# Turned outputs and rows of maxima move into the ring of three PSUM banks, and the scores use the second job bank while it is empty

## The chip, the core and the metric

One core of a Trainium2 chip runs the whole kernel as one program. The time is device microseconds of that core, the median over runs. Its engines work side by side, each in the order of its own queue, and wait for each other by semaphores: TensorE (PE, matrix products; it writes only to PSUM), VectorE (DVE), ScalarE (ACT), GpSimd (POOL) and SyncE (SP, which here issues DMAs). PSUM has eight banks of 128 partitions by 512 floats.

## The reference

For 2048 tokens of width 256, four blocks are added to the residual one after the other, each on a layer norm of the running sum:

```python
x = x + cross_attention(layernorm(x), ctx)   # 16 heads of 16, 1601 keys, softmax(scale*(tau*q.k + delta))
x = x + top1_expert(layernorm(x))            # 8 experts of 256x256, one is chosen for each token
x = x + window_attention(layernorm(x), ctx)  # keys within 16 of p_t, times a Gauss bell, tanh(cat @ W_c)
x = x + slot_ffn(layernorm(x))               # top 8 of 64 slots; a small network on the 64 slots
```

The last block needs a sum over all tokens before its output, so it has an end of its own after all tokens are through.

## The kernel before, in words

**Start.** Contexts and weights are loaded, keys and queries are projected in blocks of 512 columns (`BLOCKS`, `project`), and each block is split into three bf16 parts (`split`, or `block_mid` and `low_of`). Gathers (`move_k`, `move_q`, L525 and L533) copy the parts to the stacks from which a score product gets full precision in one pass. `START` is the order of these steps on every engine, `BESIDE` what stands beside the first 78 maxima units. There `("L", 1)` are statistics of the second tile of tokens, `("U",)` the masks of the window (`masks`, L1613 on), which wait for all constants.

**Chunks.** The tokens are cut in four chunks of 512. A chunk has 52 slots (4 groups of heads by 13 tiles of 128 keys) of 4 quarters, so 208 quarters; quarter q is head q % 4 of slot q // 4. In each quarter TensorE makes one score product (L1350, 512 columns), ScalarE its exponential (L848), and TensorE one or two maxima units (L1064, 401 columns), each reduced by VectorE (L1651). These units are for the row maxima of the group of heads that comes next. At the end of each slot comes the product of the exponentials of the slot before with the values (L1148, four heads, eight records). At the end of a group the output is copied to SBUF by ScalarE, turned by TensorE (`turn_o`, the "o") and normalised by VectorE; the 16 columns of maxima of a group are turned too (`max_rows`, the "m") and written as rows (`max_out`).

**Jobs.** While chunk c runs, the rest of the network for chunk c - 1 is done in jobs between the quarters: `behind(c)` on TensorE, VectorE and ScalarE. `JOBS` holds for each job its name, the one before it, how many quarters behind that it may start, and its hold: how many quarters it keeps its bank. ota/otb turn the attention's output, y0/y1 project it, t1, t2, t3 turn normed tokens, router and e0 to e15 are the experts (one product of 512 columns for each two experts of a tile of tokens; VectorE adds its two halves at L1788 in the quarters q + 4 and q + 5), gateT and gb0/gb1 add biases, score, aT, z are the window, h, logits, slots, alphaT the slots. `places()` gives each a quarter (`AT`).

**Banks.** Two banks hold the scores (`ps_e`), one the running output (`ps_o`), five are `ps_m`: a ring of three for maxima units, and two for jobs, which alternate. Before the change the o and m pass through the two job banks too, at fixed quarters (`O_AT` = 6, 58, 110, 162 and `M_AT` = 45, 97, 149, 201): `places()` keeps those free and lets no job span them, and `job_numbers()` counts them in the alternation. Chunk 0 has no jobs behind it, so its scores rotate over three banks, the second job bank (`ps_x`) being the third; chunks 1 to 3 use two.

**Order.** All queues are static. Before a matmul, TensorE waits for the semaphore of whoever read the bank last: `bank_free` for jobs, `max_taken` for the ring, `exp_done` for scores. VectorE handles its maxima, then the job steps of a quarter (`go_on`). It normalised the o two quarters after TensorE turned it, and wrote the m one quarter after, behind the job steps.

## Time and profile before

| | |
|---|---|
| median of 3 runs | 1088.85 us (1088.72 to 1089.68) |
| the profiled execution | 1086.41 us |
| its span, first to last instruction | 1084.4 us |
| TensorE (PE) busy | 978.2 us, 90% |
| its weight loads (PEld) | 390.6 us, 36% |
| VectorE (DVE) busy | 745.5 us, 69% |
| ScalarE (ACT) busy | 571.3 us, 53% |
| GpSimd (POOL) busy | 63.8 us, 6% |
| mean granted TensorE clock | 0.968 of full speed |

Durations in the rows further down come from the profiled execution. Matmuls are pipelined and their records overlap, so the distance between starts says more than a length.
### The profile page before, as it was taken

What the parts mean: (1) busy time and instruction counts of PE and PEld (TensorE: products, weight loads), DVE (VectorE), ACT (ScalarE), POOL (GpSimd) and SP (SyncE); (2) the same over time, 40 slices, a digit from 0 to 9 for tenths busy, and PEclk for the clock granted to TensorE, in tenths of its full rate; (3) what the DMA queues carried; (4) which work ended last, traced back from release to release, by engine and by line L of the source; (5) the groups of instructions that cost most, each with busy time, mean ns of one, the idle gap of its engine ahead of it and who ended that gap; (6) DMA issues with size and microseconds to landing.
All of it is one profiled execution on the core that took longest, in us unless ns stands there. A gap on an engine that the chain in (4) does not pass through costs nothing.

```text
span 1084.4 us, 13614 instructions
## 1 busy us (share of the span) xinstructions
PE 978.2 (90%) x4794; PEld 390.6 (36%) x4794; DVE 745.5 (69%) x1704; ACT 571.3 (53%) x1063; POOL 63.8 (6%) x91
## 2 busy tenths in 40 slices
PE   6799999999889999989889989989989999889986
PEld 3453323323333334423323333423333333334643
DVE  4688888887677777776677777776767764235634
ACT  2456766666454456665445546665445547740330
POOL 3441000000000000000000000000000000100000
PEclk9899999999899989999899989999899989999999
DMA  7936500001000000001000000001000000140022
GB/s 187 200 73 111 121 1 15 16 1 35 1 16 1 16 1 14 3 1 55 1 16 1 15 1 13 3 1 54 1 15 1 0 2 1 40 125 2 1 97 78
DMA packets 33931, 36.19 MB, mean 33 GB/s; under 512 B 6670, under 2 KB 30523, under 8 KB 33603
## 3 DMA queue, kind: packets, MB, share of 16 engines
q1 hardware_dynamic: 32542, 34.17, 12.5%
q10 hardware_dynamic: 1242, 0.90, 0.6%
q8 instruction: 38, 0.62, 0.2%
q0 software_dynamic: 80, 0.26, 0.1%
q14 instruction: 29, 0.24, 0.1%
HBM read 21.55 MB, written 7.35 MB: 27 GB/s over the span
## 4 chain that ended last, share of the span: by engine, by line
issue 51%; PE 30%; DVE 9%; DMA 2%; ACT 2%; POOL 2%; DVEq 2%; SPq 1%; POOLq 0%; ACTq 0%
PE ps_m L1064 7%; PE ps_o L1148 7%; PE ps_e L1350 5%; DVE mx L1651 4%; PE ps_e L1022 2%; DMA xres<-in_x 1%; PE ps_m L1350 1%; SPq L545 1%; PE ps_m L1168 1%; PE ps_m L1298 1%; POOL rstd L684 1%; POOL xres L735 1%; PE ps_m L1301 1%; DVE xn L1643 1%; DMA x<-xres 1%
## 5 line engine op out<-in xcount | busy, mean ns | idle before, releaser
L1651 DVE TENSOR_REDUCE mx<-ps_m 128x1 f32<-128x401 f32 x1024 | 538.3, 568 | 198.0 <-PE ps_m L1064 190.6
L848 ACT ACTIVATE probs<-ps_e 128x512 f32<-128x512 f32 (+1 forms) x763 | 437.1, 598 | 342.2 <-PE ps_e L1350 340.5
L1064 PE MATMUL ps_m<-k_stack,q_stack 99*128 99x401 bf16 x1024 | 319.4, 343 | 36.6 <-DVE mx L1651 34.9
L1350 PE MATMUL ps_e<-q_stack,k_stack 101*128 101x512 bf16 (+1 forms) x763 | 299.5, 394 | 10.9 <-ACT probs L848 8.7
L1148 PE MATMUL ps_o<-probs,v_heads 128*32 128x512 f32 (+1 forms) x1664 | 228.9, 623 | 0.0
L1350 PEld LDWEIGHTS ps_e<-q_stack,k_stack 101*128 101x128 bf16 (+1 forms) x763 | 75.9, 100 | 261.8 <-ACT probs L848 167.7
L1064 PEld LDWEIGHTS ps_m<-k_stack,q_stack 99*128 99x128 bf16 x1024 | 102.0, 100 | 183.8 <-DVE mx L1651 131.0
L1252 PE MATMUL ps_m<-expert_w,xnT 128*128 128x512 f32 x192 | 99.4, 598 | 15.2 <-DVE xb L1788 15.2
L1148 PEld LDWEIGHTS ps_o<-probs,v_heads 128*32 128x32 f32 (+1 forms) x1664 | 33.1, 109 | 60.7 <-issue 49.4
L848 ACT ACTIVATE probs<-ps_m 128x512 f32<-128x512 f32 (+1 forms) x69 | 41.6, 603 | 15.2 <-PE ps_m L1350 15.1
L1788 DVE SCALAR_TENSOR_TENSOR xb<-ps_m,hot,xb 128x256 f32<-128x256 f32 x84 | 40.6, 484 | 7.9
L1252 PEld LDWEIGHTS ps_m<-expert_w,xnT 128*128 128x128 f32 x192 | 34.2, 191 | 30.6 <-DVE xb L1788 20.4
L682 POOL TENSOR_TENSOR var_e<-mv,eps 128x4 f32<-128x4 f32 x13 | 2.6, 199 | 573.9 <-DVE mv L1737 566.6
L1403 PE MATMUL ps_m<-expert_w,xnT 128*128 128x512 f32 x64 | 29.0, 598 | 1.3 <-DVE xb L1953 1.3
L1350 PE MATMUL ps_m<-q_stack,k_stack 101*128 101x512 bf16 (+1 forms) x69 | 26.4, 383 | 0.0
L735 POOL TENSOR_TENSOR xres<-xres,bo 128x1024 f32<-128x1024 f32 x3 | 7.1, 2354 | 253.7 <-DMA xres<-in_x 253.7
L1022 PE MATMUL ps_e<-xnT,expert_w 128*128 128x512 f32 x32 | 17.2, 623 | 2.0 <-DVE work L1575 1.3
L1953 DVE SCALAR_TENSOR_TENSOR xb<-ps_m,hot,xb 128x256 f32<-128x256 f32 x28 | 13.5, 484 | 7.5 <-PE ps_m L1403 5.6
L1403 PEld LDWEIGHTS ps_m<-expert_w,xnT 128*128 128x128 f32 x64 | 11.7, 190 | 14.5 <-issue 11.0
L1298 PE MATMUL ps_m<-win_v,work 128*128 128x256 f32 x48 | 14.5, 383 | 1.5 <-ACT work L858 1.5
L1201 PE MATMUL ps_m<-ident,xn 128*128 128x128 f32 x72 | 15.0, 292 | 0.0
L1168 PE MATMUL ps_m<-wc,ident 128*128 128x512 f32 x24 | 14.6, 749 | 0.4 <-ACT alphaT L968 0.4
(333 smaller groups left out, 720.0 us busy)
## 6 DMA issues: line engine op xcount, KB each, us to landing
q_stack<-q_parts SPq DMA_DIRECT2D x78, 64.0 KB, 2.6
expert_w<-in_expert_wT SPq DMA_DIRECT2D x2, 1024.0 KB, 12.9
xres<-in_x SPq DMA_DIRECT2D x4, 512.0 KB, 3.8
x<-xres SPq DMA_DIRECT2D x4, 512.0 KB, 3.2
probs<-x SPq DMA_DIRECT2D x1, 2048.0 KB, 8.5
k_stack<-alphaT SPq DMA_DIRECT2D x10, 200.1 KB, 7.6
probs<-in_ctxT SPq DMA_DIRECT2D x3, 512.0 KB, 7.5
q_parts<-probs SPq DMA_DIRECT2D x4, 384.0 KB, 3.0
```

Source lines behind the costliest of these rows:

```text
L735: pool.tensor_tensor(xres[:], xres[:], bo0[:].unsqueeze(1).broadcast_to((P, TT, D)), ALU.add)\
L848: act.activation(probs[0:n, k % 2, h, :], score_bank(c, k, h)[0:n, :], ACT.Exp).then_inc(s["exp_done"], 1)
L1022: mm = pe.matmul(ps_e[b % 2][:, 0:n], wqkv[:, w, k, P * m:P * m + P], src[:, k, at_col:at_col + n], start=(k == 0), stop=(k == KT - 1))
L1064: pe.matmul(ps_m[:, (UNITS * n1 + u) % RING, 0:SPLIT], qst[0:MAX_ROW, g, h, P * t:P * t + P], kst[0:MAX_ROW, HG * g + h, QUARTER_START[q]: ...
L1148: mm = pe.matmul(ps_o[32 * h:32 * h + 32, :], v_sb[0:n, st, HG * g + h, :], probs[0:n, k % 2, h, :], start=(st == 0), stop=(st == ST - 1))
L1168: pe.matmul(out, ident[:], wc[:, 0:KT, :], start=True, stop=True)
L1252: mm = pe.matmul(bank(name, c), xnT[:, k, P * t:P * t + P], expert_w[:, k, CT * j:CT * j + CT], start=(k == 0), stop=(k == KT - 1))
L1298: pe.matmul(o, aT[:, k, tok:tok + P], win_v[:, k, :], start=(k == 0), stop=False)
L1350: pe.matmul(score_bank(c, k, h)[0:n, :], kst[0:ROWS, HG * g + h, P * st:P * st + n], qst[0:ROWS, g, h, :], start=True, stop=True).then_inc ...
L1403: mm = pe.matmul(half_bank(f"e{i}", h), xnT[:, k, tok:tok + P], expert_w[:, k, CT * j:CT * j + CT], start=(k == 0), stop=(k == KT - 1))
L1651: dve.tensor_reduce(mx[:, q, col:col + 1], ps_m[:, (UNITS * n1 + u) % RING, 0:SPLIT], AX.X, ALU.max)\
L1788: last = dve.scalar_tensor_tensor(out=xb[:, t, :], in0=bank(f"e{i}", c)[:, D * (e % 2):D * (e % 2) + D], scalar=hot8[:, t, e:e + 1], in1=( ...
```

## The change

The o and the m become items of the ring of three: `ring_numbers()` counts them in one order with the maxima units, the same on TensorE and VectorE, and both wait and signal on the ring's semaphores `max_ready` and `max_taken`. `places()` loses its fixed quarters, and `job_numbers()` its m and o. VectorE handles the m and the o in the quarter in which TensorE turns them, ahead of the job steps of that quarter. `score_plan()` chooses for every score of all chunks the bank whose last score is longest ago: out of three when no job holds the second job bank or takes it in the next quarter, else out of the two `ps_e`. A score in the third bank waits that the last job there is taken; a job in that bank waits for the exponential of the last score there.

At the start the first block of queries is projected before the third and fourth block of keys, the gathers of the first 1024 columns of keys go in two pieces of 512, the first by SyncE alone, and the first normalisation comes after the first block of keys on ScalarE. The second tile's statistics and the masks are done before the first maximum; the two constants that the masks need are loaded early under a semaphore of their own, and GpSimd's `scale_shift(1)` is moved with them.

```diff
-BLOCKS = ([("K", i, 0) for i in range(N_COLS)] + [("Q", 0, 0), ("Q", 0, 1)] + [("K", i, 1) for i in range(N_COLS)]
+BLOCKS = ([("K", 0, 0), ("K", 1, 0), ("Q", 0, 0)] + [("K", i, 0) for i in range(2, N_COLS)] + [("Q", 0, 1)]
+          + [("K", i, 1) for i in range(N_COLS)]
...
-HALVES = ((0, 2 * CT, 1), (2 * CT, S, N_COLS - 1))
-GATHER_SP, GATHER_ACT = (0, 4, 2), (1, 5, 3)
-START = [("D",), ("L", 0), ("C",), ("N", 0), ("K", 0, 0), ("S",), ("K", 1, 0), ("T", 0), ("K", 2, 0), ("K", 3, 0), ("G", 0),
-         ("Q", 0, 0), ("g",), ("G", 1)]
-START += [("V", i) for i in range(V_EARLY)]
+KEY_PIECES = ((0, CT, ("K", 0, 0)), (CT, 2 * CT, ("K", 1, 0)), (2 * CT, S, ("K", N_COLS - 1, 0)))
+HALF_OF_PIECE = (0, 0, 1)
+GATHER_SP = ((0, 4, 2, 1, 5, 3), (0, 4, 2, 1), (0, 4, 2))
+GATHER_ACT = ((), (5, 3), (1, 5, 3))
+START = [("D",), ("L", 0), ("C",), ("K", 0, 0), ("N", 0), ("S",), ("K", 1, 0), ("T", 0), ("Q", 0, 0), ("G", 1), ("K", 2, 0), ("g",),
+         ("K", 3, 0), ("V", 0), ("V", 1), ("G", 2)]
+START += [("V", i) for i in range(2, V_EARLY)] + [("L", 1), ("U",)]
...
 def places():
-    fixed = sorted([(q, q + 3) for q in O_AT] + [(q, q + 2) for q in M_AT])
     ring, at = [(0, 0), (0, 0)], {}
     for name, after, lag, hold in JOBS:
-        q = at[after] + lag if after else lag
-        while True:
...
+        q = max(at[after] + lag if after else lag, ring[-2][1])
...
 def job_numbers():
+    order = [(name, c) for c in range(NC - 1) for name in AT]
+    return {job: (1 - i % 2, i // 2) for i, job in enumerate(order)}
+
+def ring_numbers():
+    order = []
+    for v in range(UNITS + LEAD):
+        if v == UNITS + 3:
+            order.append(("m", 0))
+        order.append(divmod(v, UNITS))
     for c in range(NC):
         for q in range(HG * SLOTS):
+            k, h = divmod(q, HG)
+            order += [(NG * c + j, u) for j, u in units_at(k, h) if wanted(NG * c + j)]
             if q in M_AT and wanted(NG * c + 1 + M_AT.index(q)):
                 order.append(("m", NG * c + 1 + M_AT.index(q)))
             if q in O_AT and (c or q > O_AT[0]):
                 order.append(("o", NG * c + O_AT.index(q) - 1))
...
+def score_plan():
+    hold = {name: h for name, _, _, h in JOBS}
+    jobs = [(HG * SLOTS * (c + 1) + AT[name], name, c) for name, c in JOB if JOB[name, c][0] == 1]
+    plan, last, last_score = [], [None] * 3, {}
+    for n in range(HG * SLOTS * NC):
+        near = any(at <= n + 1 and n < at + hold[name] for at, name, _ in jobs)
+        b = min(range(2 if near else 3), key=lambda i: -1 if last[i] is None else last[i])
+        begun = [(name, c) for at, name, c in jobs if at < n]
+        plan.append((b, last[b], begun[-1] if begun else None))
+        last[b] = n
+        last_score.update({(name, c): last[2] for at, name, c in jobs if at == n})
+    return plan, last_score
...
         def bank_free(eng, job, c):
             b, n = JOB[job, c]
             need(eng, bank_taken[b], n)
+            if b and LAST_SCORE[job, c] is not None:
+                eng.wait_ge(s["exp_done"], LAST_SCORE[job, c] + 1)
...
         def score_bank(c, k, h):
-            return ps_e[h % 2] if c else (*ps_e, ps_x)[(HG * k + h + 1) % 3]
+            return (*ps_e, ps_x)[SCORES[HG * (SLOTS * c + k) + h][0]]
...
+            sp.dma_start(iota_w[:], io["c_iota"].partition_broadcast(P)).then_inc(s["ld_masks"], 16)
+            sp.dma_start(slotT[:], io["slot_initT"].rearrange("(k p) n -> p k n", p=P)).then_inc(s["ld_masks"], 16)
...
             pool.memset(eb[:], 0.0).then_inc(s["fills_set"], 1)
+            scale_shift(1)
...
                     for h in range(HG):
-                        need(pe, s["exp_done"], HG * SLOTS * c + HG * k + h - (1 if c else 2))
+                        b, last, job = SCORES[HG * (SLOTS * c + k) + h]
+                        if last is not None:
+                            pe.wait_ge(s["exp_done"], last + 1)
+                        if b == 2 and job:
+                            wait_taken(pe, *job)
...
             def masks():
-                dve.wait_ge(s["ld_const"], N_CONST)
+                dve.wait_ge(s["ld_masks"], 32)
...
                                 if u == UNITS - 1:
                                     max_columns()
-                        if h == 0 and st == 2 and (g or c):
+                        if HG * k + h in M_AT and wanted(NG * c + max_end(k - 1)):
+                            j = max_end(k - 1)
+                            need(dve, m_loaded[(j - 1) % NG], 32 * (c + (j - 1) // NG + 1))
+                            max_out(NG * c + j)
+                        if HG * k + h in O_AT and (g or c):
                             if g == 1 and c:
                                 wait_filled(dve, "y1", c - 1)
                             normalise(NG * c + g - 1)
                         go_on(work, HG * k + h)
```

## Rows read from the trace of the kernel before

**Rows 1.** busy time by stage, its first line naming the columns
```profile
core 0: us, PE busy (x) PEld busy (x) DVE busy (x) ACT busy (x) POOL busy (x), PEclk, DMA share, GB/s
...
91.50:250.00 158.50, 154.87 (x888) 47.53 (x888) 133.49 (x276) 109.07 (x211) 0.61 (x1) 1.00 0.22 41
250.00:493.00 243.00, 222.56 (x1123) 85.83 (x1119) 176.46 (x393) 133.06 (x243) 5.98 (x7) 0.96 0.04 11
493.00:734.80 241.80, 221.11 (x1123) 85.04 (x1119) 176.10 (x392) 132.73 (x243) 5.98 (x7) 0.97 0.04 12
734.80:966.00 231.20, 209.98 (x1052) 79.39 (x1048) 136.00 (x311) 132.33 (x243) 8.33 (x8) 0.96 0.04 13
```

**Rows 2.** waits in the stretch 493:734.8: us in total, times, longest
```profile
DVE mx L1651 <- PE ps_m L1064: 56.4, 67, 2.7
...
PE ps_m L1064 <- DVE mx L1651: 9.8, 18, 1.8
...
PE ps_m L1252 <- DVE xb L1788: 5.1, 4, 1.6
```

**Rows 3.** timeline, a slot with experts: start us, us, instruction
```profile
335.68 0.39 PE L1350 MATMUL ps_e<-q_stack,k_stack 101*128 101x512 bf16 x1
...
337.50 0.38 PE L1350 MATMUL ps_e<-q_stack,k_stack 101*128 101x512 bf16 x1
...
337.53 1.06 DVE L1651 TENSOR_REDUCE mx<-ps_m 128x1 f32<-128x401 f32 x2
338.68 0.48 DVE L1788 SCALAR_TENSOR_TENSOR xb<-ps_m,hot,xb 128x256 f32<-128x256 f32 x1
...
339.24 1.07 PE L1148 MATMUL ps_o<-probs,v_heads 128*32 128x512 f32 x8
340.24 0.39 PE L1350 MATMUL ps_e<-q_stack,k_stack 101*128 101x512 bf16 x1
```

**Rows 4.** timeline, TensorE at an expert that waits for its bank
```profile
561.74 1.12 PE L1252 MATMUL ps_m<-expert_w,xnT 128*128 128x512 f32 x2 [1.51 <-DVE xb L1788]
```

**Rows 5.** timeline, hand-overs at quarters 13 and 18 of chunk 2
```profile
504.31 0.38 PE L1350 MATMUL ps_e<-q_stack,k_stack 101*128 101x512 bf16 x1
...
504.67 0.58 ACT L858 COPY attn_chunk<-ps_m 128x512 f32<-128x512 f32 x1
...
511.54 0.38 PE L1350 MATMUL ps_e<-q_stack,k_stack 101*128 101x512 bf16 x1
...
511.68 0.68 DVE L1725 TENSOR_TENSOR xa<-xres,ps_m 128x512 f32<-128x512 f32 x1
```

**Rows 6.** timeline, bare slots at the end of chunk 3
```profile
927.80 0.70 PE L1350 MATMUL ps_e<-q_stack,k_stack 101*128 101x512 bf16 x2
...
928.94 0.88 PE L1350 MATMUL ps_e<-q_stack,k_stack 101*128 101x512 bf16 x2 [0.44 <-ACT probs L848]
...
930.75 0.61 PE L1350 MATMUL ps_e<-q_stack,k_stack 101*128 101x512 bf16 x2
```

**Rows 7.** busy time of a slot of chunk 2 with maxima and statistics
```profile
694.20:698.30 4.10, 3.21 (x21) 0.77 (x17) 4.01 (x13) 2.28 (x4) 1.21 (x2) 1.00 0.00 0
```

**Rows 8.** timelines and busy time around the masks
```profile
33.86 0.58 DVE L1651 TENSOR_REDUCE mx<-ps_m 128x1 f32<-128x401 f32 x1 [10.44 <-PE ps_m L1064]
...
41.73 0.34 PE L1064 MATMUL ps_m<-k_stack,q_stack 99*128 99x401 bf16 x1 [0.83 <-DVE mx L1651]
...
53.66 0.52 PE L1064 MATMUL ps_m<-k_stack,q_stack 99*128 99x401 bf16 x1 [4.39 <-DVE mx L1651]
...
53.66:58.50 4.84, 4.65 (x9) 2.21 (x10) 4.17 (x13) 0.37 (x1) 1.81 (x5) 0.50 1.06 150
```

**Rows 9.** DMA issues by shape: count, KB each, median us to landing
```profile
k_stack<-k_stack SPq DMA_DIRECT2D x3, 128.0 KB, 6.7
...
k_stack<-k_stack SPq DMA_DIRECT2D x3, 72.1 KB, 4.9
```

**Rows 10.** busy time of the stretch that holds the wait at 561.74
```profile
558.00:575.00 17.00, 14.65 (x75) 5.15 (x68) 10.76 (x22) 7.96 (x15) 0.00 (x0) 1.00 0.00 1
```

More of the change, by code:

```diff
@@ L149, in places @@
 def places():
-    fixed = sorted([(q, q + 3) for q in O_AT] + [(q, q + 2) for q in M_AT])
     ring, at = [(0, 0), (0, 0)], {}
     for name, after, lag, hold in JOBS:
-        q = at[after] + lag if after else lag
-        while True:
-            while fixed and fixed[0][0] < q:
-                ring.append(fixed.pop(0))
-            q = max(q, ring[-2][1])
-            if not fixed or fixed[0][0] >= q and ring[-1][1] <= fixed[0][0]:
-                break
-            q = max(q, fixed[0][0] + 1)
+        q = max(at[after] + lag if after else lag, ring[-2][1])
         at[name] = q
@@ L180, in job_numbers @@
                 order.append(("o", NG * c + O_AT.index(q) - 1))
-        if c == 0:
-            first = len(order)
-        else:
-            order += [(name, c - 1) for name in AT if AT[name] >= HG * SLOTS]
     order.append(("o", NG * NC - 1))
-    numbers = {job: (0, i) for i, job in enumerate(order[:first])}
-    numbers.update({job: (1 - i % 2, i // 2 + (first if i % 2 else 0)) for i, job in enumerate(order[first:])})
-    return numbers
+    return {item: i for i, item in enumerate(order)}
 def begin(steps):
@@ L398, in build @@
         k_loaded = [sem(f"k_loaded{g}") for g in range(NG)]
-        k_half = [sem(f"k_half{i}") for i in range(len(HALVES))]
+        k_half = [sem(f"k_half{i}") for i in range(2)]
         q_loaded = [sem(f"q_loaded{g}") for g in range(NG)]
@@ L611, in _ @@
                 sp.wait_ge(q_stored[m], 16 * NC)
-            for half in k_half:
-                sp.wait_ge(half, 16 * K_PARTS)
+            for i, half in enumerate(k_half):
+                sp.wait_ge(half, 16 * K_PARTS * HALF_OF_PIECE.count(i))
             sp.wait_ge(k_loaded[1], 16 * K_PARTS)
@@ L1057, in max_unit @@
                 if n1 == 0 and u % (UNITS // 2) == 0:
[L1058 removed]
+                    half = u // (UNITS // 2)
+                    pe.wait_ge(k_half[half], 16 * K_PARTS * HALF_OF_PIECE.count(half))
                 if u == 0:
@@ L1070, in max_rows @@
                 pe.wait_ge(s["mx_ready"], n1 + 1)
-                bank_free(pe, "m", n1)
-                filled(pe.transpose(bank("m", n1)[0:HG * TT, 0:P], mxc[:], ident[:]), "m", n1)
+                ring_free(pe, ("m", n1))
+                pe.transpose(ring_bank(("m", n1))[0:HG * TT, 0:P], mxc[:], ident[:]).then_inc(s["max_ready"], 1)
             def step(kind, *args):
@@ L1462, in _ @@
             for b in range(2):
-                pe.wait_ge(bank_taken[b], 1 + max(n for bank_no, n in JOB.values() if bank_no == b))
-            pe.wait_ge(s["max_taken"], UNITS * NG * NC)
+                pe.wait_ge(bank_taken[b], sum(bank_no == b for bank_no, _ in JOB.values()))
+            pe.wait_ge(s["max_taken"], len(RING_NO))
             turned_half("ot", 0, att)
@@ L1659, in max_out @@
             def max_out(n1):
-                wait_filled(dve, "m", n1)
-                dve.tensor_scalar(mrow[:, 0, :], bank("m", n1)[0:HG * TT, 0:P], -1.0, None, ALU.mult)
+                wait_ring_filled(dve, ("m", n1))
+                turned = ring_bank(("m", n1))[0:HG * TT, 0:P]
+                dve.tensor_scalar(mrow[:, 0, :], turned, -1.0, None, ALU.mult)
                 dve.drain()
-                taken(dve.scalar_tensor_tensor(out=mrow[:, 1, :], in0=bank("m", n1)[0:HG * TT, 0:P], scalar=-1.0,
-                                               in1=mrow[:, 0, :], op0=ALU.mult, op1=ALU.subtract), "m", n1)
+                dve.scalar_tensor_tensor(out=mrow[:, 1, :], in0=turned, scalar=-1.0, in1=mrow[:, 0, :],
+                                         op0=ALU.mult, op1=ALU.subtract).then_inc(s["max_taken"], 1)
             def step(kind, *args):
@@ L1714, in normalise @@
                         dve.wait_ge(k_loaded[g], 16 * k_loads(g))
-                turned = bank("o", n).rearrange("p (t j e) -> p t j e", t=TT, j=HG)
+                turned = ring_bank(("o", n)).rearrange("p (t j e) -> p t j e", t=TT, j=HG)
                 dve.reciprocal(z_inv[:], turned[:, :, :, E])
```

85 lines of the change are left out of this document (45 added, 40 removed).

## The prediction

> **What bounds the kernel now.** I read the busy time by stage first. From 91.5 us on, four chunks of 52 slots take 158.5, 243.0, 241.8 and 231.2 us, and TensorE is busy 98, 92, 91 and 91% of them; VectorE is behind it with 73%, ScalarE with 55% [rows 1]. So TensorE sets the time, and what can change is its stalls and the stretches at the lower clock. The waits of one chunk name two kinds that end at VectorE: 18 waits for a maxima bank, 9.8 us, and 4 waits for an expert's bank, 5.1 us [rows 2]. The timeline says what a slot (four quarters) looks like while experts run: one slot from 335.68 to 340.24 is 4.56 us, filled but for the last tenth, with its values product of 1.07 us at the end [rows 3]. The same rows hold what matters most here: the third quarter's score starts at 337.50, but VectorE ends the second quarter's expert work only at 338.68 + 0.48 = 339.16, after two maxima of 1.06 us. VectorE runs 1.66 us behind TensorE at that point, and it costs nothing, since no one asks for that bank before the next quarter but one.
>
> **The plan that comes out of the change.** Following the planner's rules with the fixed places gone: e2 moves from quarter 48 to 46, e5 from 64 to 60, e13 from 98 to 92, gb0 from 112 to 104, and everything after it is 8 quarters earlier. Of the 208 scores of a chunk with jobs behind it, 41 go to the third bank. The rule takes the bank whose last score is oldest, so the third bank is taken at once when its job's hold has passed: an expert at quarter q has hold 6, and the score at q + 6 goes there. It waits for that expert's bank to be taken, which VectorE does in quarter q + 5. For e6, e8, e10, e12 and e14 (64, 72, 80, 88, 96) that score is at 70, 78, 86, 94 and 102, each the third quarter of a slot: exactly the place of the row at 337.50.
>
> **Chunks 1 to 3, new waits.** Each of the five costs 339.16 - 337.50, with the release some 1.7 us: 8.5 us. The row says such a wait is real: an expert that asks one quarter after the last take of its bank, at 561.74, stood 1.51 us for it [rows 4]. The score at 62 waits for e4, by the same rows about 1.4, since TensorE has there done a turned output more. The score at 48 waits for e1 behind a values product of 1.07 us [rows 3] (0.4 left), gb1 at 106 for e15 (1.7 less 0.39 for the score and maxima ahead of it: 1.3), the score at 108 for gb0 (0.3). Sum 11.9 us a chunk; bounds 8.5 and 14, because a VectorE that is ahead by one finished wait could shave the next.
>
> The other hand-overs of the third bank ask in the same way one quarter after the take. In today's trace the score at quarter 13 starts at 504.31 and ScalarE's copy of ota ends at 505.25 (0.9 us); at quarter 18 the score starts at 511.54 and the sum of y0 ends at 512.36 (0.8) [rows 5]. t1a at quarter 31 is a copy as ota's. With the release, 1.0, 0.9 and 0.9. Five more of this shape (router at 35, score0 at 125, z0 at 151, t3a at 173, slots at 201) I estimate at 0.5 to 1.0 each, 3.5 together. Where a wait for the same engine follows closely, part is paid already: I take 5.5 of 6.3. Bounds 2 (VectorE is the slower one around them anyway) and 7.
>
> **What goes.** The four expert waits: e2, e5 and e13 no longer come behind an m; e4 moves from the third to the first quarter of a slot, behind a values product of 1.07 us, which covers it. That is -5.1 us a chunk [rows 2]. The wait of gb0 (-0.5) and ota's wait for the output normalised two quarters later (-0.3) go with it. The third bank elsewhere: without it the score at 928.94 stands 0.44 us behind an exponential, and the slot from 927.80 to 930.75 takes 2.95 us [rows 6]; with one more bank the fourth score waits where the third does, 0.5 us less a slot. Where maxima run, the free slots are VectorE's: 4.01 us busy of 4.10 [rows 7], so a third bank buys little; I take -1.5 a chunk over some 8 slots. In chunk 3 maxima end at slot 36, and nine slots gain 0.5 more: -4.5 there. Bounds of what goes: -5 and -9.
>
> The o and m items now take two places of the ring's order. VectorE handles o two quarters earlier and stands for the transposes; the next maxima, and with them TensorE's ring, are queued behind it. It idles 56.4 us of the chunk for maxima [rows 2], so this costs 0; without that cover it is about 0.5 us for each of four. The bank's wait on exponentials asks for a score at least two quarters old, done by then: 0. Since each new wait gives VectorE time, I take 1 us a chunk off the 9.8 us of ring waits.
>
> Net: 11.9 + 5.5 - 5.1 - 0.8 - 1.5 - 1.0 = +9.0 for chunks 1 and 2, +4.5 for chunk 3: **+22.5 us**. Chunk 0 already rotates three banks: 0.
>
> **Before the chunks.** The masks and the second tile's statistics move ahead of the first maximum, where VectorE is idle for 10.44 us waiting for it; the work is about as long as the two stalls below, and hides there. In the loop they made TensorE stand 4.39 us at 53.66 and 0.83 at 41.73, and after the first the granted clock was 0.50 for the 4.84 us from 53.66 to 58.50, which costs half of that, 2.4 [rows 8]. Sum -7.6, and the row of maxima one unit earlier -0.4: **-8**. What is late next is VectorE's own maxima, 78 x 0.5 us, with some 4 us of slack over the shortened loop. The new order of blocks readies the first queries some 3 us earlier (two blocks of keys, each a pass of VectorE over 512 columns, come behind them now), but the first maximum starts with the last gather, and there are now 12 key pieces of 64 KB in place of 6 of 128 KB. A gather of 128 KB lands in 6.7 us and one of 72 KB in 4.9 [rows 9]: halving the size saves a quarter of the time and doubles the number, up to 3 us later; the earlier queries give up to 3 back. I take 0, bounds -3 and +3. SyncE also issues two loads (mask indices, slots) earlier, 1.2 us ahead of gathers that wait for another store anyway. Bounds of the whole part: -11 and 0.
>
> The Trainium skill, page "DMA: Bandwidth & Descriptors", section "Why small descriptors are slow (HBM only)", says that transfers from SBUF to SBUF don't suffer from small pieces. By it the split gathers would cost nothing and the first maximum would be up to 3 us earlier; the two rows on the gathers disagree with it in part.
>
> **Sum.** +22.5 - 8 = +14.5 us on the profiled execution's 1086.41 us (span 1084.4), 1100.9. That run was 2.4 us under the median of the timed ones, so I expect **1103 us**. With all bounds one way: chunks +1, start -11, about 1079; the other way +43 and 0, about 1132. Its own range is 1090 to 1118.
>
> **Rivals.**
> - *The third bank pays and its waits are covered (faster), 0.19.* If VectorE comes to the expert work sooner than today, so that each new wait is half as long (6.0), and the hand-overs lie in slots that VectorE sets anyway (1.0), a chunk is 6.0 + 1.0 - 8.4 = -1.4, chunk 3 -5.9, and with -8 it is -17: 1072 to 1080, say 1075. For it: the row of 4.01 of 4.10. Against: the two maxima that delay the expert's take are issued by TensorE only in the quarter just before. The point from which it decides: new waits below 12.6 us a chunk of my 17.4.
> - *The clock falls in the expert stretch (slower still), 0.10.* If half of the 18 expert waits are each followed by a stretch like that after 53.66 (4.84 us at half clock, 2.4 us lost), +22: 1125. For it: 4.39 us of idle was followed by one. Against: waits of 1.5 us in the stretch from 558 to 575 ran at 1.00 throughout [rows 10]. The Trainium skill, page "TensorE: Matmul & The Clock Gate", section "A second HAM failure mode: psum-queue depth-cycling", describes just this: a kernel that cycles PSUM banks idles briefly so often that the clock swings. By that rule it is 1125, by the row nothing.
> - *The change doesn't do what it says, 0.02*: third-bank scores too few to show, the start alone, 1081.
>
> The forecast has 0.69. The range 1085 to 1119 holds it nearly whole and a small part of the first rival. A difference of 0.2% (2.2 us) is about what can be told from none: faster 0.19, within 0.04, slower 0.77.
>
> **What would show it.** Right: score matmuls (L1350's line) idle for VectorE's expert sum, 18 times about 1.5 us; expert products waiting for an expert's bank nearly gone; slots 17 to 25 alternating 4.6 and about 6.2 us; the first score some 8 us before 91.5, at about 83.5; bare slots of chunk 3 at 2.4 us. Wrong: if slots 17 to 25 stay at 4.6 us, the new waits are not there and the first rival holds; if the mean granted clock of chunks 1 to 3 falls below today's 0.96 to 0.97 by more than 0.02, the second.

## The result and the profile after

The changed kernel took 1118.97 us (median of 4 runs, 1118.25 to 1122.76) beside 1089.03 for the kernel before on the same chip: a ratio of 1.0281, 95% interval 1.0257 to 1.0305. It is slower, as forecast, but by 30 us where 14.5 were forecast: at the upper edge of the range of 1085 to 1119, and just above the forecast's own 1090 to 1118. The profiled execution of after took 1118.63 us, its span is 1116.6, so 32.2 us of span have to be found against before's 1084.4.

Busy time by stage of the kernel after, from its first score on; the columns are as in [rows 1]:

```profile
88.30:248.50 160.20, 156.75 (x890) 46.60 (x889) 134.21 (x277) 109.74 (x212) 1.09 (x1) 1.00 0.22 41
248.50:505.20 256.70, 223.06 (x1123) 85.84 (x1119) 176.76 (x393) 133.26 (x243) 6.00 (x7) 0.96 0.03 9
505.20:761.70 256.50, 222.88 (x1123) 85.27 (x1119) 176.82 (x393) 132.97 (x243) 5.99 (x7) 0.96 0.04 11
761.70:999.40 237.70, 206.10 (x1036) 78.21 (x1032) 136.92 (x312) 130.52 (x241) 8.34 (x8) 0.96 0.04 13
```

TensorE's work in chunks 1 and 2 is the same to 2 us (222.6 and 221.1 before), as is VectorE's. The stages grew by waiting, 13.7 and 14.7 us. The last chunk of [rows 1] was drawn to 966, 2.3 us past its last score; by score to score it was 228.8, so chunk 3 grew by 8.8.

The waits of TensorE in chunk 2 of the kernel after, to be held against [rows 2] (us in total, times, longest). L1394 is the score, L1104 the maxima product, L1833 the expert sum, L1292 the expert product, L1197 the turned output:

```profile
PE ps_m L1394 <- DVE xb L1833: 10.7, 7, 1.8
PE ps_m L1104 <- DVE mx L1695: 10.0, 17, 1.8
PE ps_m L1394 <- ACT xnT L897: 1.8, 2, 0.9
PE ps_m L1394 <- ACT hT L943: 1.6, 1, 1.6
PE ps_m L1197 <- DVE mx L1695: 1.2, 2, 1.0
...
PE ps_m L1394 <- DVE slot_acc L1911: 1.1, 1, 1.1
PE ps_m L1394 <- ACT attn_chunk L897: 0.9, 1, 0.9
PE ps_m L1394 <- DVE lg L1799: 0.9, 1, 0.9
PE ps_m L1394 <- DVE xa L1770: 0.8, 1, 0.8
PE ps_m L1394 <- ACT work L935: 0.7, 1, 0.7
...
PE ps_m L1394 <- DVE work L1770: 0.5, 1, 0.5
PE ps_m L1292 <- DVE xb L1833: 0.2, 1, 0.2
```

Every row of L1394 with a reader other than the exponential is a score in the third bank: 19.0 us in 16 waits, seven of them behind experts. The expert product's own wait, 5.1 in [rows 2], is 0.2. The ring's wait for maxima stayed, 10.0 against 9.8.

One such wait on the timeline of the kernel after, in the third quarter of a slot as in [rows 3]:

```profile
601.43 0.38 PE L1394 MATMUL ps_e<-q_stack,k_stack 101*128 101x512 bf16 x1
601.44 0.48 DVE L1833 SCALAR_TENSOR_TENSOR xb<-ps_m,hot,xa 128x256 f32<-128x256 f32 x1
601.65 0.51 PE L1104 MATMUL ps_m<-k_stack,q_stack 99*128 99x401 bf16 x2
601.85 0.60 ACT L887 ACTIVATE probs<-ps_e 128x512 f32<-128x512 f32 x1 [0.59 <-PE ps_e L1394]
602.02 1.06 DVE L1695 TENSOR_REDUCE mx<-ps_m 128x1 f32<-128x401 f32 x2
603.17 0.48 DVE L1833 SCALAR_TENSOR_TENSOR xb<-ps_m,hot,xb 128x256 f32<-128x256 f32 x1
603.80 0.38 PE L1394 MATMUL ps_m<-q_stack,k_stack 101*128 101x512 bf16 x1 [1.64 <-DVE xb L1833]
```

VectorE takes half of the expert at 601.44, then two maxima, then the other half at 603.17; only 0.15 us after that has ended does the score start. The profile calls 1.64 us idle; the slot as a whole is 1.80 longer than one without it. From score to score, slots 15 to 25 of chunk 2 took 6.36, 4.56, 6.36, 4.56, 6.36, 4.56, 6.36, 4.56, 8.20, 5.00 and 6.37 us: the alternation that the forecast named. The 8.20 is the wait at quarter 94 with a stretch at half clock behind it.

The start. TensorE's first maxima on its timeline, in the kernel before and in the kernel after:

```profile
33.50 0.50 PE L1064 MATMUL ps_m<-k_stack,q_stack 99*128 99x401 bf16 x2
36.25 0.83 PE L1104 MATMUL ps_m<-k_stack,q_stack 99*128 99x401 bf16 x2 [7.79 <-DMA q_stack<-probs]
```

From there to the first score it is 52.0 us, before 58.0. So the masks' stalls of [rows 8] did go, but 2.75 us of the gain was paid before the loop: the first score is at 88.27 instead of 91.51.

### The profile page after: what moved, and what is told of

It reads as the page before. It is cut to its first block, busy times and chain, and to the rows that moved or that the text cites. A ratio compares the mean times of both kernels' runs of the same rounds, so it can differ in the third digit from the quotient of the medians.

```text
span 1116.6 us, 13781 instructions
## 1 busy us (share of the span) xinstructions
PE 974.1 (87%) x4794; PEld 386.3 (35%) x4794; DVE 746.5 (67%) x1704; ACT 571.5 (51%) x1063; POOL 64.4 (6%) x91
## 4 chain that ended last, share of the span: by engine, by line
issue 50%; PE 29%; DVE 8%; DMA 4%; SPq 3%; ACT 2%; POOL 2%; DVEq 1%; POOLq 0%; ACTq 0%
PE ps_m L1104 7%; PE ps_o L1188 7%; DVE mx L1695 5%; PE ps_e L1394 5%; PE ps_m L1394 2%; DMA xres<-in_x 2%; PE ps_e L1061 1%; SPq L578 1%; DMA q_stack<-probs 1%; DMA d_parts<-delta_parts 1%; POOL rstd L721 1%; POOL xres L773 1%; PE ps_m L1341 1%; DVE xn L1687 1%; PE ps_m L1338 1%
## 5 line engine op out<-in xcount | busy, mean ns | idle before, releaser
L887 ACT ACTIVATE probs<-ps_e 128x512 f32<-128x512 f32 (+1 forms) x640 | 370.3, 599 | 293.3 <-PE ps_e L1394 291.7
L1104 PE MATMUL ps_m<-k_stack,q_stack 99*128 99x401 bf16 x1024 | 318.9, 343 | 40.3 <-DVE mx L1695 30.9
L1394 PE MATMUL ps_e<-q_stack,k_stack 101*128 101x512 bf16 (+1 forms) x640 | 249.3, 391 | 2.5 <-ACT probs L887 2.3
L1104 PEld LDWEIGHTS ps_m<-k_stack,q_stack 99*128 99x128 bf16 x1024 | 101.4, 99 | 194.4 <-DVE mx L1695 136.4
L887 ACT ACTIVATE probs<-ps_m 128x512 f32<-128x512 f32 (+1 forms) x192 | 115.1, 599 | 101.0 <-PE ps_m L1394 100.8
L1394 PEld LDWEIGHTS ps_e<-q_stack,k_stack 101*128 101x128 bf16 (+1 forms) x640 | 64.1, 100 | 199.7 <-ACT probs L887 116.4
L1394 PE MATMUL ps_m<-q_stack,k_stack 101*128 101x512 bf16 (+1 forms) x192 | 75.7, 394 | 56.2 <-DVE xb L1833 32.1
L1292 PE MATMUL ps_m<-expert_w,xnT 128*128 128x512 f32 x192 | 99.8, 601 | 0.7 <-DVE xb L1833 0.7
L1394 PEld LDWEIGHTS ps_m<-q_stack,k_stack 101*128 101x128 bf16 (+1 forms) x192 | 19.2, 100 | 123.0 <-issue 61.8
L1833 DVE SCALAR_TENSOR_TENSOR xb<-ps_m,hot,xb 128x256 f32<-128x256 f32 x84 | 40.6, 483 | 7.8
L1292 PEld LDWEIGHTS ps_m<-expert_w,xnT 128*128 128x128 f32 x192 | 35.1, 193 | 12.5 <-DVE xb L1833 2.1
L1061 PE MATMUL ps_e<-xnT,expert_w 128*128 128x512 f32 x32 | 17.3, 628 | 2.9 <-issue 2.9
L1998 DVE SCALAR_TENSOR_TENSOR xb<-ps_m,hot,xb 128x256 f32<-128x256 f32 x28 | 13.6, 484 | 7.5 <-PE ps_m L1447 5.6
L813 ACT ACTIVATE work<-ps_e,cond 128x512 f32<-128x512 f32 (+1 forms) x11 | 7.2, 653 | 21.0 <-PE ps_e L1061 21.0
L1447 PEld LDWEIGHTS ps_m<-expert_w,xnT 128*128 128x128 f32 x64 | 11.7, 190 | 14.4 <-issue 11.0
L1338 PE MATMUL ps_m<-win_v,work 128*128 128x256 f32 x48 | 14.5, 383 | 1.6 <-issue 1.6
```

Source lines behind the costliest of these rows:

```text
L887: act.activation(probs[0:n, k % 2, h, :], score_bank(c, k, h)[0:n, :], ACT.Exp).then_inc(s["exp_done"], 1)
L1061: mm = pe.matmul(ps_e[b % 2][:, 0:n], wqkv[:, w, k, P * m:P * m + P], src[:, k, at_col:at_col + n], start=(k == 0), stop=(k == KT - 1))
L1104: pe.matmul(ring_bank((n1, u))[:, 0:SPLIT], qst[0:MAX_ROW, g, h, P * t:P * t + P], kst[0:MAX_ROW, HG * g + h, QUARTER_START[q]:QUARTER_STA ...
L1292: mm = pe.matmul(bank(name, c), xnT[:, k, P * t:P * t + P], expert_w[:, k, CT * j:CT * j + CT], start=(k == 0), stop=(k == KT - 1))
L1338: pe.matmul(o, aT[:, k, tok:tok + P], win_v[:, k, :], start=(k == 0), stop=False)
L1394: pe.matmul(score_bank(c, k, h)[0:n, :], kst[0:ROWS, HG * g + h, P * st:P * st + n], qst[0:ROWS, g, h, :], start=True, stop=True).then_inc ...
```

## The experiments

All times are compared with the kernel before, run on the same chip; across chips its median was 1087.0 to 1089.0. Chunk lengths are from first score to first score in each profiled run (the last one to its last score). "Half clock" is a granted clock of 0.50; where a stretch is bound by TensorE, a microsecond of it costs up to 0.5 us against full clock.

**e1: the scores keep two banks.** What is left of the change is the ring with o and m in it, the new places, and the start.

```diff
-        near = any(at <= n + 1 and n < at + hold[name] for at, name, _ in jobs)
+        near = n >= HG * SLOTS
```

> The kernel after, but in chunks 1 to 3 the scores use their own two banks alone; o and m stay in the ring, the start is the new one. Theory H (the third bank costs the time: each first score in it behind a job waits for the job's last reader): all hand-over waits go, 20.9 us in chunk 2 of the trace after, while what stays of the change is the start (-3.2), chunk 0 (+1.7), the waits of pairs and experts for the expert sum that are gone (-5.1 in each of chunks 1 to 3) and the ring's new waits (+1.6 in each); about 1089 - 3.2 + 1.7 + 3 x (-3.5) = 1077 us, between 1072 and 1082, and PE's idle in front of scores put down to the expert sum below 1 us in a chunk. Theory R (the ring with two more users costs the time, through the maxima that wait): above 1100 us. Theory C (the granted clock, whose half stretches moved): 1089 or more, with as many half-clock stretches as after.

Measured 1070.34 us, ratio 0.9829 (0.9794 to 0.9864). The change minus the third bank is *faster* than before by 1.7%. Chunks 1 to 3 took 237.0, 238.0 and 222.5 us against 243.0, 241.7 and 228.8 before, so the ring with its two more users, and the places that it frees, give 16.2 us; with the third bank they took 256.8, 256.5 and 237.6: the bank costs 19.7, 18.6 and 15.2 us, 53.4 in all. Theory R falls, and so does theory C: these chunks hold 44.4 us at half clock in e1 and 58.0 in the kernel after, so the clock can be at most 6.8 of the 53.4. The waits of TensorE in chunk 2 of e1, with no score behind a job any more:

```profile
PE ps_m L1104 <- DVE mx L1695: 9.0, 18, 1.8
PE ps_e L1394 <- ACT probs L887: 1.8, 5, 0.8
```

It is also 2 us below my range: I had counted 3.5 us a chunk for the ring and it is 5.4.

**e2: behind an expert the third bank opens one quarter later.**

```diff
-        near = any(at <= n + 1 and n < at + hold[name] for at, name, _ in jobs)
+        near = any(at <= n + 1 and n < at + hold[name] + (name[0] == "e") for at, name, _ in jobs)
```

> The kernel after, but behind an expert the third bank opens to the scores one quarter later (gb and the other jobs as they were). Theory H: of the 20.9 us of hand-over waits in a chunk the seven behind experts go (1.8 x 5 + 0.7 + 1.8 = 11.5 us; q94's 2.0 among them), in three chunks 34: 1085 us, between 1080 and 1091, because a quarter more (1.15 us) covers most of a wait of 1.8 and leaves 0.7 at each that takes the bank then. Theory R or C: no change, 1115 or more.

Measured 1088.81 us (ratio 1.0008, 0.9991 to 1.0025), 30 us under after and within the range. In its trace the 0.7 us that I had left at each place is gone too, for a reason that I had not seen in the plan: one quarter later the next expert of that bank is due at once (`at <= n + 1`), so between two experts of the second bank the third bank isn't taken at all, 34 scores a chunk instead of 41. e2 takes the seven hand-overs out rather than making them late. (That it is still 4 us longer than expected goes with its clock, 0.964 on average over its runs where after has 0.968; the last section has what that costs.) The timeline of e2, the same slot as above:

```profile
585.61 0.48 DVE L1833 SCALAR_TENSOR_TENSOR xb<-ps_m,hot,xa 128x256 f32<-128x256 f32 x1
...
586.17 0.38 PE L1394 MATMUL ps_e<-q_stack,k_stack 101*128 101x512 bf16 x1
...
586.19 1.06 DVE L1695 TENSOR_REDUCE mx<-ps_m 128x1 f32<-128x401 f32 x2
...
587.35 0.48 DVE L1833 SCALAR_TENSOR_TENSOR xb<-ps_m,hot,xb 128x256 f32<-128x256 f32 x1
587.42 0.38 PE L1394 MATMUL ps_e<-q_stack,k_stack 101*128 101x512 bf16 x1
...
588.90 0.39 PE L1394 MATMUL ps_e<-q_stack,k_stack 101*128 101x512 bf16 x1
```

All four scores are in ps_e, the scores' own banks. The one at 586.17 starts 0.56 us behind its neighbour; the sum of the expert ends at 587.83, 1.66 us later, while TensorE has other work, and nobody waits for it.

**e3: the third bank serves at the seven scores behind experts alone.**

```diff
+        near = n >= HG * SLOTS and not any(name[0] == "e" and n == at + hold[name] for at, name, _ in jobs)
+        near = near or any(at <= n + 1 and n < at + hold[name] for at, name, _ in jobs)
```

> The kernel after, but in chunks 1 to 3 the third bank serves only at the seven scores right behind an expert (q48, 62, 70, 78, 86, 94, 102); everywhere else two banks. Theory H, waits add up: e1's time plus 3 x 11.5 = 34, less what the third bank gives back at the next score (0.3 us each at most): 1106 to 1112 us. Rival W (the waits of the score are made good later, since VectorE, which is late, catches up while PE stands): e1 plus less than 20, below 1097.

Measured 1105.14 us (1.0166, 1.0126 to 1.0205), 34.8 above e1 and 1 us under my range; by the traces the chunks are 12.3, 11.2 and 13.3 us longer, 36.7 together, for idle time of 10.7 us a chunk behind the expert sum, twenty-one waits in all. The waits are not made good later; rival W (less than 20 us over e1) falls.

Not all of the 36.7 is waiting. At full clock the slots of the seven hand-overs are 11.7 us a chunk longer than e1's, 35.0 in three. But the wait at quarter 94, the longest with 1.85 us, was followed by half clock in each of e3's three chunks; this is the first of them:

```profile
367.50:370.90 3.40, 3.40 (x12) 0.51 (x10) 1.01 (x2) 0.89 (x2) 0.00 (x0) 0.50 0.00 0
```

That slot took 8.19 us in every chunk, and 6.56 where the clock stayed up (chunks 1 and 3 of after): 4.9 us in three. The other slots came out 3.2 shorter than e1's.

The remaining third-bank scores, e2 against e1, cost 6.8, 4.4 and 6.1, 17.3 us (with 6.8 us more at half clock than e1, so up to 3.4 of it may be the clock's). The two parts add up to 54.0, where the bank costs 53.4.

**e4: the old start under the new ring and third bank.** The order of blocks, the six larger gathers and the masks in the first loop are those of before:

```diff
-KEY_PIECES = ((0, CT, ("K", 0, 0)), (CT, 2 * CT, ("K", 1, 0)), (2 * CT, S, ("K", N_COLS - 1, 0)))
+HALVES = ((0, 2 * CT, 1), (2 * CT, S, N_COLS - 1))
...
+            BESIDE += [(SPACE * i - 8, ("U",)), (SPACE * i + 2, ("u",))]
```

> The kernel after with the start of the kernel before (order of blocks, gathers, masks in the first loop), ring and third bank as after. If the start is worth what the two traces show up to the first score (-3.2 us): 1122 us. If it is worth more and chunk 0 hides it (-3.2 + 1.7): 1120. If the whole -8 of the forecast is there and something else took it: 1127. None of the theories on the third bank expects a change elsewhere.

Measured 1127.42 us (1.0350, 1.0314 to 1.0386), which reads like the forecast's full 8 us. Its trace says otherwise: of 11.5 us of span more than after, 5.6 lie before the first score (93.9 against 88.3), 1.0 in the chunks, and 4.9 in the tail, whose instructions are the same. Busy time of the tail, of e4 first:

```profile
1006.10:1128.10 122.00, 101.56 (x370) 55.88 (x369) 59.29 (x176) 24.95 (x50) 6.22 (x14) 0.94 0.22 67
```

and of the kernel after:

```profile
999.40:1116.60 117.20, 96.06 (x370) 52.06 (x370) 59.30 (x176) 24.96 (x50) 6.23 (x14) 0.99 0.22 70
```

Besides TensorE's own two columns (matmuls and weight loads) only the granted clock moved, 0.94 against 0.99. The 5.6 before the first score are not free of it either: e4 has 17.1 us at half clock there, after and before 10.2 each, so up to 3.4 of them may be the clock's. Chunk 0 is 160.2 us with the old start as with the new (before: 158.6), so its +1.6 doesn't come with the start.

**e5: the two halves of the expert sum are issued together on VectorE.**

```diff
-                        yield AT[f"e{i}"] + 4 + e % 2
+                        yield AT[f"e{i}"] + 4
```

> The kernel after with one edit on VectorE alone: the second half of each expert's sum is issued right behind the first half, a quarter earlier, so before the two or three maxima that stood between them. Theory O (the 1.8 us of a score behind an expert is the sum's place in VectorE's order): in the trace after the second half ran at 603.17 to 603.65, behind two maxima of 0.57 us and PE's own standing, and the score came at 603.80; without the two maxima it ends at about 602.5 and the score comes near 602.65: each wait of 1.8 falls to 0.7, five or six in a chunk, -6 us a chunk, -18 in all: 1101 us, between 1097 and 1107, as far as the maxima that now come 0.5 us later don't hold PE. Rival P (the wait is the depth of the pipeline from PE's last matmul over VectorE to the score, wherever the sum stands, or the maxima made later cost PE as much): within 3 us of 1119.

Measured 1092.13 us (1.0042, 1.0021 to 1.0063), 27 us under after; the estimate was 18 and the edge of its range 22. Its profiled execution is one of the long ones, 1099.82 us; in it the chunks are 12.9, 6.6 and 5.8 us shorter than after's, 25.3 together. Waits in chunk 2 of e5:

```profile
PE ps_m L1104 <- DVE mx L1695: 10.1, 17, 1.8
PE ps_m L1394 <- DVE xb L1833: 3.2, 6, 0.9
```

The sum's wait fell from 10.7 to 3.2 us a chunk, 22.5 in three, and the maxima that now run later cost nothing. On e5's timeline the score stands 0.47 us instead of 1.64:

```profile
586.71 0.48 DVE L1833 SCALAR_TENSOR_TENSOR xb<-ps_m,hot,xa 128x256 f32<-128x256 f32 x1
...
587.27 0.48 DVE L1833 SCALAR_TENSOR_TENSOR xb<-ps_m,hot,xb 128x256 f32<-128x256 f32 x1
587.67 1.53 DVE L1695 TENSOR_REDUCE mx<-ps_m 128x1 f32<-128x401 f32 x3
...
587.90 0.38 PE L1394 MATMUL ps_m<-q_stack,k_stack 101*128 101x512 bf16 x1 [0.47 <-DVE xb L1833]
```

So the wait was the sum's place in VectorE's order, and not the work: the same instructions in another order.

**e6: the third bank two quarters behind every job** (25 scores a chunk instead of 41).

```diff
+        near = any(at <= n + 1 and n < at + hold[name] + 2 for at, name, _ in jobs)
```

> The kernel after, but behind every job of the second bank the scores take the third bank only two quarters later than the job's planned end (25 scores in a chunk instead of 41, none between two experts). Theory H (only the hand-over costs; where it is covered the third bank gives what it gave in the bare slots, 2.46 against 2.95 us): e1's 1070.3 less about 4 in the last slots of chunk 3 and 0.5 in each chunk's first slots: 1065 us, between 1061 and 1069. Rival B (a third bank is of no use in a chunk whose bound is VectorE's maxima): 1070, the same as e1. Rival N (hand-overs cost even when late, by the wait itself): over 1075.

Measured 1062.71 us (0.9769, 0.9756 to 0.9783), 7.6 under e1: the third bank does give something where its hand-over is covered. Chunks: 235.9, 234.8, 219.3, that is 1.1, 3.2 and 3.1 less than e1, of which the clock can be 1.7 (41.0 us at half clock against 44.4). In chunk 3, slot 41 took 2.46 us in e6 and 2.95 in e1, slot 40 took 2.82 and 3.26. In the kernel after those slots were as short, but the slots of hand-overs between them lost it again: slots 36 to 51 together took 58.1 us before, 56.7 after and 55.7 in e1. Waits of e6 in chunk 2:

```profile
PE ps_m L1104 <- DVE mx L1695: 10.3, 17, 1.8
```

**e7 and e8: SP gathers before it waits for delta's parts,** on e1 and on e6.

```diff
-            sp.wait_ge(s["delta_stored"], 16)
-            sp.dma_start(kst[DELTA_ROW:DELTA_ROW + 3, 0:3 * HG, :], d_parts[:, 0:S].unsqueeze(1).broadcast_to((3, 3 * HG, S)))\
-              .then_inc(s["ld_delta_k"], 16)
...
             first_keys(0)
             first_keys(1)
+            sp.wait_ge(s["delta_stored"], 16)
+            sp.dma_start(kst[DELTA_ROW:DELTA_ROW + 3, 0:3 * HG, :], d_parts[:, 0:S].unsqueeze(1).broadcast_to((3, 3 * HG, S)))\
+              .then_inc(s["ld_delta_k"], 16)
```

> e1 (two score banks in chunks 1 to 3) with one edit of the start: SP's wait for delta's parts in DRAM, 12.9 to 19.1 us of the trace after, and the load behind it come after the ten gathers of the first two key blocks, whose parts were ready at 13.99 and 16.36. Theory S (the gathers' issue on SP sets the first maximum): gathers are issued 14.0 to 20.5, q's 20.9 to 22.8 instead of 25.8 to 28.0; the first maximum comes near 31 instead of 36.2 and the time falls by 5: 1065 us, between 1062 and 1068. Rival L (the last DMA of the run lands late whatever its issue; or delta's rows, which now land last, set the first maximum): between 1068 and 1072.

> e6 and e7 together: if both hold, 1060 us, between 1055 and 1064; if the start gives nothing, as e6.

Measured 1069.57 (0.9839, 0.9814 to 0.9864) and 1061.66 us (0.9749, 0.9726 to 0.9772): 0.8 and 1.0 us under e1 and e6, nothing that can be told in the times (in the traces the first score came 3.2 and 2.6 us earlier). The gathers were issued from 14.0 on as planned, but the first maximum only moved to 35, behind what now came last. TensorE first stood at the projection ahead of it, as e7's waits before the chunks say:

```profile
PE ps_e L1061 <- DMA k_stack<-d_parts: 7.6, 1, 7.6
```

The gathers of the queries were complete at 34.07 in e8, 9.98 us after the last one was issued by SP; in the kernel after that was 8.7 (27.41 to 36.12). The miss is Theory S's: the issue was not the only thing that set the first maximum.

**e9: delta's rows by head group,** 38 KB for the first group right behind the first key block, on e6.

```diff
+            def delta_rows(g, done):
+                sp.dma_start(kst[DELTA_ROW:DELTA_ROW + 3, g * HG:(g + 1) * HG, :],
+                             d_parts[:, 0:S].unsqueeze(1).broadcast_to((3, HG, S))).then_inc(done, 16)
             first_keys(0)
+            sp.wait_ge(s["delta_stored"], 16)
+            delta_rows(0, s["ld_delta_k"])
             first_keys(1)
```

> e6 (third bank two quarters behind every job) with the start changed again: SP gathers the first key block before it waits for delta's parts, and delta's rows of the key stack are loaded by head group, the first group's third (38 KB instead of 113) right behind the first block's gathers, the other two behind the gathers of the queries. In e7 and e8 the first maximum waited 7.6 and 8.0 us for the load of delta's rows (issued at 21.7 and 22.6), and q's last gather landed at 34.07. Theory D (the size and place of delta's load set the first maximum): it no longer ends last; the first maximum comes with q's last gather, 2 us earlier at the most if that still lands near 34 and up to 6 if the gather was late only behind delta's load: e6's 1062.7 less 1.5 to 6, 1057 to 1061. Rival L (the last gather of a set lands late in any case, as in all four traces so far): first maximum at 33.5 or later, 1060 to 1063.

Measured 1056.94 us (0.9728, 0.9704 to 0.9752), 5.8 under e6, at the lower edge of my range. The first maximum is at 31.56 (e8: 34.87), the first score at 84.35, 4.7 earlier than e6's. Of the wait of 7.6 us there remain

```profile
PE ps_m L1110 <- DMA q_stack<-probs: 3.1, 1, 3.1
...
PE ps_e L1067 <- DMA k_stack<-d_parts: 1.7, 1, 1.7
```

**e10: a margin of one quarter, with e5's order of the sum.**

```diff
+        near = any(at <= n + 1 and n < at + hold[name] + 1 for at, name, _ in jobs)
...
+                        yield AT[f"e{i}"] + 4
```

> The kernel after with the third bank one quarter behind every job and the expert sums issued together (as in e5), so more scores take the third bank than in e6, with every wait of e5 (0.9 at most behind an expert, 1.6 behind gelu) shorter by the quarter of 1.1 to 1.5 us. Theory M (what counts is that the hand-over is covered; a margin of one does where the reader is prompt): between 1060 and 1066, as e6. Rival V (VectorE's maxima are the bound between experts, and sums issued together delay them): PE's waits for maxima, 10 us in chunk 2 in all kernels so far, grow, 1068 or more.

Measured 1057.58 us (0.9715, 0.9692 to 0.9738), below the range, with SP's order as in after. Chunks 233.0, 233.0, 218.2. By the plan 28 scores a chunk are in the third bank, again none between experts, so the early sum could save no hand-over of a score here. TensorE's wait for maxima did grow, to 11.5 us, and of the hand-overs the one behind job h (ScalarE's gelu, L943) is left:

```profile
PE ps_m L1104 <- DVE mx L1695: 11.5, 19, 1.8
PE ps_m L1197 <- DVE mx L1695: 1.5, 3, 1.0
PE ps_m L1394 <- ACT hT L943: 1.1, 1, 1.1
```

Of the 5.8 us that the chunks are shorter than e6's, the clock can hold most: they have 30.7 us at half clock, e6's 41.0. Whether the margin of one or the early sum gives the rest was not separated.

**e11: e10 with e9's start.**

> e10 with e9's start. If the two gains are of different stretches they add: e10's 1057.6 less what e9 gained over e6 (5.8): 1052 us, between 1049 and 1055. If the start's gain goes into clock phases or chunk 0: 1056 or more.

Measured 1053.06 us (1049.53 to 1057.42; ratio 0.9680, 0.9650 to 0.9709): 3.2% faster than before and 66 us under after. The same parts as in the change, with the third bank opened a quarter later (and so never between experts), the sum issued together, and delta's load split. Part of it may be the clock: the mean over its runs is 0.974, over before's on that chip 0.967.

**e12: the change's start alone, on the kernel before.** It adds to before what e4 takes from after (the diff of e4 the other way).

> The kernel before with the change's start alone (blocks, gathers, masks ahead of the first loop); ring, job banks and score banks as before. By the stretch up to the first score in the two traces the start is worth 3.2 us, by e4 against after (93.9 against 88.3) 5.6: before less 3.2 to 5.6, a ratio of 0.995 to 0.997. Rival: the forecast's 8 us, 0.9925; or nothing beyond noise, 0.999 or more, if chunk 0's 1.7 us of after came with the start.

Measured 1082.74 us (0.9952, 0.9924 to 0.9979): 5.2 us, with the first score at 88.83. It agrees with e4's 5.6; the interval (2.3 to 8.3 us) holds both the 3.2 of the two traces and the forecast's 8. The runs of e12 had a mean clock of 0.970 and before's 0.967, worth 2 to 3 us by the last section (an estimate), so the 3.2 of the two traces, which hold 10.2 us at half clock each up to the first score, is the best figure. Chunk 0 is 158.6 us in its trace, as before, which puts the 1.7 us of after's chunk 0 on the ring.

## Why the forecast was right in sign and short in size

The step that failed is the sum of sizes, not the mechanism: the third bank, at +43.2 us, was sized 10 us too low; the ring was given a gain that isn't there; and two places were put at 0 that cost time, what stands before the first maximum and chunk 0. All misses but the tail's went the same way.

By its own terms, forecast and measured (spans of the profiled runs; the third bank's part is after less e1, the ring's is e1 less before, in chunks 1 to 3):

| term | forecast | measured |
|---|---|---|
| third bank in chunks 1 to 3: 3 x (11.9 + 5.5 - 1.5) - 4.5 | +43.2 | +53.4 |
| ring and places in chunks 1 to 3: 3 x (-5.1 - 0.8 - 1.0) | -20.7 | -16.2 |
| start up to the first score | -8 | -3.2 |
| chunk 0 | 0 | +1.7 |
| tail | 0 | -3.5 |
| sum | +14.5 | +32.2 |

The tail's -3.5 is luck: its instructions are the same, and it has 12.1 us at half clock in before's trace and 2.1 in after's. Without it the miss would be larger.

**The mechanism was right.** A hand-over is on the path as soon as someone asks for the bank at once. What was named came: 18 expert waits that lengthen their slots by 1.8 to 2.0 us (forecast 1.7), the seven places, the alternation of 4.6 and 6.36 us, the vanished waits of the expert product. e2, e3 and e5 show it by three different edits.

**The third bank was undersized by 10 us.** Three things go into it.

- The experts: 10.3 a chunk in the sum (the 11.9 without gb1 and q108), 11.7 by the slots of e3; q94 and q62 took 2.0 and 1.8 where 1.7 and 1.4 stood. Against that, of the 1.6 for gb1 and q108 only 0.2 came, so the two nearly cancel.
- The other hand-overs, the weak step: I took 5.5 a chunk, and in chunk 2 TensorE stood 8.3 us for them. Router, score0, z0, t3a and slots lengthened the way from one score to the next by 1.0, 0.7, 0.8, 1.1 and 1.2 us against e1, 4.8 where I had "3.5 together", and the score at 180 (1.68), which waits for ScalarE's gelu of job h, was not in the list at all. I had sized them all from two rows of other jobs [rows 5].
- The clock: 13.6 us more at half clock in chunks 1 to 3 than e1 has, at most 6.8 of the 53.4. How much of the miss is this and how much the waits, single traces don't separate.

**The catch-up of VectorE (-1.0 a chunk) doesn't exist.** "Each new wait gives VectorE time" was argued without a row. The ring's wait for maxima is 10.0 after and 9.8 before (9.0 in e1), so it did not fall by 1.0. A reason can be argued, not shown: while TensorE stands, it issues no maxima products either, so VectorE gains nothing on it. In e3 the waits cost their full length. Without this term the ring would have been forecast at -5.9 a chunk; it measured -5.4.

**The start: the loop nearly as forecast, what stands before it not.** I expected -8 from the loop and it gave -6.0, with 3.0 us at half clock in it against 6.8 before. The step "I take 0, bounds -3 and +3" for the first maximum came out at +2.75: SP was blocked until 19.07 on delta's store, then issued 13 gathers of about 0.64 us each, the queries' last as the thirteenth. In the kernel before it was the sixth, and SP began with the queries' gathers at 23.46; in the kernel after at 25.82, 2.4 us later. I had called these "gathers that wait for another store anyway" and so seen the wait, but not that twice the number of gathers stood behind it, nor that the store itself stood behind the two early loads: it was issued at 11.36 instead of 9.50, and SP came free at 19.07 instead of 18.20. The half-sized gathers landed in 4.6 us at the median (10 of 64 KB from SP), where the 128 KB ones took 6.7 [rows 9], so what I had from the sizes holds.

The Trainium skill ("DMA: Bandwidth & Descriptors", "Why small descriptors are slow (HBM only)") says that transfers from SBUF to SBUF don't pay the penalty of small descriptors. I had read it as "splitting costs nothing". It speaks of the data's way alone; here the issue counted, 0.64 us for each gather, one after another on one queue.

**Chunk 0 was called 0 and is +1.7.** There VectorE is busy 84% of the time where it is 73% in chunk 2, and TensorE 98% [rows 1], so a new wait has no cover. The row of maxima waits for the ring, four times 0.2 in the view below, and the turned output three times. By slots, the four rows cost 0.48 us each, 1.9; the three outputs cost 0.42 each but the slot behind each is 0.66 shorter; the first two slots are 0.5 longer. Kernel after, waits of TensorE from 88 to 250 us:

```profile
PE ps_m L1104 <- DVE mx L1695: 1.8, 4, 0.5
PE ps_m L1112 <- DVE mx L1695: 0.8, 4, 0.2
PE ps_m L1197 <- DVE mx L1695: 0.7, 3, 0.2
```

I had used the idle time of VectorE in chunk 2 [rows 2] as cover for a chunk that doesn't have it.

**The rivals.** "Waits covered" had its decision at 12.6 us of new waits a chunk; they were 19.0. The clock: TensorE's mean granted clock in chunks 1 to 3 was 0.96, 0.96, 0.96, within 0.01 of before. One expert wait, the 1.85 us at quarter 94 of chunk 2, was followed by half clock, in busy time of the kernel after:

```profile
622.10:626.30 4.20, 2.35 (x10) 1.04 (x10) 2.77 (x6) 1.25 (x3) 0.00 (x0) 1.00 0.00 0
626.30:629.70 3.40, 3.40 (x13) 0.66 (x11) 1.15 (x2) 1.14 (x2) 0.00 (x0) 0.50 0.00 0
```

The other expert waits of this kernel passed at full clock. The experiments say more. In after, e3 and e4 together, which all have these hand-overs, 6 of the 9 waits of 1.85 us at quarter 94 were followed by half clock within 0.8 us, and none of the 45 waits of 1.64 us. So the danger that the rival named is real for the longest wait alone. The Trainium skill ("TensorE: Matmul & The Clock Gate", "A second HAM failure mode: psum-queue depth-cycling") would have had many of them swing; by these traces most don't, and each that did cost about 1.6 us (slot 23 took 8.20 us in chunk 2 of after and 6.56 in chunks 1 and 3). In all, chunks 1 to 3 of after hold 58.0 us at half clock and those of before 47.8. Ten us more at half clock is at most 5 of the 32 us; e1, with 44.4, is as near to before in this as it is far from after in time. Why the other stretches fall where they do stays open.

## What to carry to other kernels

A buffer that is reused at once puts its last reader's place in the *reader's* program order on the critical path of the engine that asks for it, however idle the buffer looks in a plan. Before giving a spare bank to the engine that sets the time, read on the timeline when the previous user's last reader ends, and open the bank only where that is past: leaving out seven such hand-overs of a chunk was worth 30 us here, and issuing the two halves of one sum side by side, on an engine with time to spare, 27. And a part of a change that looks harmful as a whole may hide a gain: without its worst part this one was 1.7% faster than before.

## What the runs showed of the hardware

The time of one kernel on one chip follows the granted clock closely. Runs of e12 went from 1074.55 us at a mean granted clock of 0.980 over 1080.2 at 0.972 and 1083.87 at 0.969 to 1089.12 at 0.962: some 0.8 us for each thousandth. The tail, the same work in every kernel, shows it in the small: it took 116.9 to 117.2 us with 2.1 to 2.3 us at half clock (three traces), 120.0 with 8.8, 120.5 to 120.8 with 10.7 to 12.1 (four), and 121.8 to 122.4 with 14.1 to 15.2 (six), about 0.4 us for each us at half clock. So a stage that an edit doesn't touch can differ by 5 us between two profiles, and a smaller difference between two stages of single profiled runs says little until their time at half clock has been compared.

A set of gathers is complete long after its last issue: in the kernel after 8.7 us after SP's last gather of the queries, in e8 9.98, though the ones ahead of it are shown with 5.5 and 3.3 to 3.7. These shorter figures are not each gather's own. The six gathers of a set share one semaphore, and its count is dealt out in the order of issue, so what is slow in any of them shows at the last. Only the completion of the set is certain, and what holds it was not tried.
